# A new start for a fused feed-forward, attention and feed-forward kernel: loads, halving, bias and beta, and the orders of the first batch

## What is computed

```
ln(x)  = (x - mean) / sqrt(var + eps)
ffn(x) = (ln'(ln(x)) * gamma + beta) @ w_q.T + bias      # ln': once more, w_q = ternary(weight)
x = x + 0.5 * ffn(x)
x = x + attn(ln(x))          # 16 query heads, 4 key and value heads of 128, rotary positions,
                             # causal, window of 64, projection Wo, biases bq, bk, bv, bo
x = x + 0.5 * ffn(x)
```

## Time and profile before

| | |
|---|---|
| Median of 3 runs | 799.77 us (799.43 to 799.82) |
| The profiled execution | 799.18 us, of it 797.4 us span |
| TensorE busy | 782.2 us, 98% of the span |
| VectorE, ScalarE, GpSimd busy | 624.6, 468.2, 459.6 us |
| Mean granted TensorE clock | 0.993 |

### The profile page before, as it was taken

How to read it: one execution, slowest core, us unless ns; L and a number is a source line. 1 busy time by engine, 2 the same in 40 slices (tenths; PEclk the granted TensorE clock), 3 DMA queues, 4 the chain that set the end, 5 groups by cost and what they waited for, 6 DMA issues and landing times.

```text
span 797.4 us, 16145 instructions
## 1 busy us (share of the span) xinstructions
PE 782.2 (98%) x5658; PEld 731.4 (92%) x5658; DVE 624.6 (78%) x1325; ACT 468.2 (59%) x1595; POOL 459.6 (58%) x470
## 2 busy tenths in 40 slices
PE   6999999999999999999999999999999999999997
PEld 5788999999999999999999999999999999999996
DVE  4778967978679886888778887797867988687756
ACT  3176565656646576465656556465664657655573
POOL 3668743866357664467446674476635766446343
PEclk7999999999999999999999999999999999999999
DMA  8292425333243422524244242533324342243400
GB/s 297 53 232 62 94 50 137 80 94 80 54 120 93 126 48 58 154 67 109 52 97 116 64 110 53 134 81 87 86 55 120 93 121 52 54 106 75 113 14 27
DMA packets 54353, 74.11 MB, mean 93 GB/s; under 512 B 7168, under 2 KB 30208, under 8 KB 54272
## 3 DMA queue, kind: packets, MB, share of 16 engines
q1 hardware_dynamic: 53712, 72.74, 37.1%
q10 hardware_dynamic: 560, 0.34, 0.1%
HBM read 14.33 MB, written 4.19 MB: 23 GB/s over the span
## 4 chain that ended last, share of the span: by engine, by line
PE 93%; DVE 3%; issue 1%; POOL 1%; DMA 1%; ACT 1%; ACTq 0%; POOLq 0%; DVEq 0%
PE job_p L649 32%; PE attn_p L649 23%; PE scores_p L666 13%; PE heads_p L649 11%; PE probsT_p L728 7%; PE job_p L823 4%; PE job_p L801 2%; DMA columns_s<-columns 1%; PE job_p L814 1%; POOL q_s L1233 0%; DVE q_s L932 0%; PE heads_p L867 0%; ACT probs L1106 0%; DVE parts L998 0%; POOL probs L1222 0%
## 5 line engine op out<-in xcount | busy, mean ns | idle before, releaser
L649 PE MATMUL attn_p<-wo_s,headsT 128*128 128x256 f32 x1536 | 209.0, 286 | 1.5 <-ACT headsT L1127 1.5
L649 PE MATMUL job_p<-xnT,wq_s 128*128 128x512 f32 x768 | 205.9, 403 | 0.8 <-DVE v_s L938 0.5
L649 PEld LDWEIGHTS attn_p<-wo_s,headsT 128*128 128x128 f32 x1536 | 196.4, 190 | 7.2 <-ACT headsT L1127 2.2
L1106 ACT ACTIVATE probs<-scores_p,neg_max 128x96 f32<-128x96 f32 x512 | 168.0, 352 | 53.4 <-DVE neg_max L887 53.4
L1233 POOL TENSOR_TENSOR q_s<-q_s,rope_swap 128x512 f32<-128x512 f32 x128 | 164.2, 1291 | 47.8 <-DMA rope_swap<-rope_sin 47.5
L1222 POOL TENSOR_TENSOR probs<-probs,inv_sum 128x384 f32<-128x384 f32 x128 | 107.2, 838 | 140.8 <-DVE inv_sum L893 140.8
L1127 ACT ACTIVATE headsT<-heads_p,columns_s 128x512 fp32r<-128x512 f32 x128 | 88.2, 689 | 134.7 <-PE heads_p L649 134.3
L649 PEld LDWEIGHTS job_p<-xnT,wq_s 128*128 128x128 f32 x768 | 135.7, 189 | 26.2 <-DVE k_s L932 1.1
L921 DVE SCALAR_TENSOR_TENSOR rope_sin<-job_p,columns_s,rope_t 128x512 f32<-128x512 f32 x160 | 119.1, 744 | 21.8 <-PE job_p L649 21.4
L666 PE MATMUL scores_p<-k_s,q_s 128*128 128x96 f32 (+2 forms) x1024 | 131.6, 272 | 0.0
L666 PEld LDWEIGHTS scores_p<-k_s,q_s 128*128 128x128 f32 x1024 | 126.7, 192 | 2.5 <-POOL q_s L1233 0.2
(11 more groups left out here) (91 smaller groups left out, 981.7 us busy)
## 6 DMA issues: line engine op xcount, KB each, us to landing
rope_swap<-rope_sin SPq DMA_DIRECT2D x320, 128.0 KB, 2.4
v_odd<-v_s SPq DMA_DIRECT2D x64, 192.0 KB, 3.3
x_in<-x SPq DMA_DIRECT2D x15, 256.0 KB, 3.4
out<-x_res SPq DMA_DIRECT2D x15, 256.0 KB, 2.5
x_tr<-x_transposed SPq DMA_DIRECT2D x7, 512.0 KB, 5.3
q_s<-wq SPq DMA_DIRECT2D x3, 512.0 KB, 10.3
q_s<-wo SPq DMA_DIRECT2D x2, 512.0 KB, 10.6
x_res<-wo SPq DMA_DIRECT2D x2, 512.0 KB, 5.9
```

The source lines that it names most:

```text
L649: mm = nc.tensor.matmul(dst, a(p), b(q), start=clears and i == 0, stop=len(pairs) == 1, skip_group_check=True)
L1106: ins = nc.scalar.activation(probs[:, i, k, 0:REACH], scores_p[i][:, k, 0:REACH], ACT.Exp, bias=neg_max[:, i, k:k + 1], accum_out=row_sum[ ...
```

## The change

- ScalarE issues the columns first, then x_in blocks 2 and 3, then the identity.
- ScalarE halves gamma (gamma0i); beta is no longer halved. GpSimd loses gamma0i, half0i and the bias step of half 0.
- ScalarE makes y of batch 0, both halves, from shift and rstd. The one semaphore y_ready becomes two, one for each half of the y buffer.
- The beta matmuls in the banks of the first batch are gone. One product in attn_p sums bias (by the identity) and beta (by the ternary weights), ahead of the first FO. VectorE reads it: bias_first adds half of it to half 0 of x_in, fold_beta writes half of it to half_b. GpSimd adds half_b to half 1 as before.
- The tables of the prologue and of the first batch are new for all engines, the fills are (10, 2, 1, 3, 3). The tables of the middle and last batches are unchanged.

```diff
-FILLS = (10, 1, 1, 2, 6, 6)
+FILLS = (10, 2, 1, 3, 3)
...
+FIRST_BIASED = numbered(DVE_STEPS, "bias1")
...
-        y_ready = sem("y_ready")
+        y_ready = [sem(f"y_ready{i}") for i in range(2)]
...
                     else:
-                        pe.wait_ge(bias_ready, 2)
+                        pe.wait_ge(bias_ready, 1)
+                        if FIRST_BIASED:
+                            pe.wait_ge(first_biased, len(FIRST_BIASED))
...
-                if x[2] == 0 and x[0] == "FO1":
-
+                if FFN_OUT[x] == 0:
 
                     pe.wait_ge(tern_ready, 1)
-                    for k in range(2):
-                        for e in range(EC):
-                            nc.tensor.matmul(bank[:, k * E:(k + 1) * E], beta_s[:, e:e + 1].to_broadcast([P, P]),
-                                             w_tern[:, e, :].bitcast(F32), start=k == 0 and e == 0, stop=False,
-                                             skip_group_check=True)
...
             def beta_product(_):
 
+                pe.wait_ge(ident_in, 16)
+                pe.wait_ge(rows_in, 16)
+                nc.tensor.matmul(attn_p[0][:, 0, :], identf[:, :], half_b, start=True, stop=False)
+                pe.wait_ge(columns_in, 16)
                 pe.wait_ge(tern_ready, 1)
-                pe.wait_ge(gamma_ready, 1)
                 for e in range(EC):
                     mm = nc.tensor.matmul(attn_p[0][:, 0, :], beta_s[:, e:e + 1].to_broadcast([P, P]),
-                                          w_tern[:, e, :].bitcast(F32), start=e == 0, stop=e == EC - 1)
+                                          w_tern[:, e, :].bitcast(F32), start=False, stop=e == EC - 1)
                 mm.then_inc(beta_ready, 1)
...
                 dve.wait_ge(beta_ready, 1)
-                dve.wait_ge(biased["1"], 2)
-                nc.vector.tensor_tensor(half_b, attn_p[0][:, 0, :], half_b, ALU.add).then_inc(bias_ready, 1)
+                nc.vector.tensor_scalar(half_b, attn_p[0][:, 0, :], 0.5, None, ALU.mult).then_inc(bias_ready, 1)
+
+            def bias_first(x):
+
+                m = x[1]
+                wait_y(dve, Y_HALVES["YT1", m, 0])
+                dve.wait_ge(beta_ready, 1)
+                nc.vector.scalar_tensor_tensor(
+                    out=x_in[:, 2 * m:2 * m + 2, :], in0=attn_p[0][:, 0:1, :].to_broadcast([P, 2, E]), scalar=0.5,
+                    in1=x_in[:, 2 * m:2 * m + 2, :], op0=ALU.mult, op1=ALU.add).then_inc(first_biased, 1)
...
+            def halve_gamma(_):
+
+                act.wait_ge(columns_in, 16)
+                nc.scalar.activation(gamma_s, gamma_s, ACT.Copy, scale=0.5).then_inc(gamma_ready, 1)
...
+            act.dma_start(columns_s[:, :], columns).then_inc(columns_in, 16)
             act.dma_start(x_in[:, 2:4, :], x_t[0][:, 2:4, :]).then_inc(x_loaded[1], 16)
             act.dma_start(identf[:, :], ident).then_inc(ident_in, 16)
-            act.dma_start(columns_s[:, :], columns).then_inc(columns_in, 16)
...
-            def halve_gamma(_):
-
-                pool.wait_ge(columns_in, 16)
-                nc.gpsimd.tensor_scalar(gamma_beta, gamma_beta, 0.5, None, ALU.mult).then_inc(gamma_ready, 1)
-
-            def halve_bias(_):
-                pool.wait_ge(rows_in, 16)
-                nc.gpsimd.tensor_scalar(half_b, half_b, 0.5, None, ALU.mult).then_inc(bias_ready, 1)
```

In the first batch's tables SyncE loads x_tr ahead of the swap of key 1 and x_in behind that of query 6; TensorE has S3 ahead of O0 and Q9 ahead of T2; GpSimd has pad0i behind the rope additions and Q7 ahead of probs2; ScalarE has w9 ahead of w11:

```diff
     "first": """
-        K1c loadt0n Q4c load0n Q5c Q6c stage9f Q7c K2c Q8c Q9c Q10c Q11c K3c
+        loadt0n K1c Q4c Q5c Q6c load0n Q7c K2c stage9f Q8c Q9c Q10c Q11c K3c
```

More of the change, by code:

```diff
@@ L61 @@
     "prologue": """
-        fill0i total0i fill1i YT0n YT1n fill2i FO0n fill3i FO1n gsum0i open0i fill4i XT0n beta0i
-        fill5i XT1n V00n K0n Q0n Q1n Q2n Q3n V01n
+        fill0i total0i fill1i YT0n YT1n beta0i FO0n gsum0i fill2i FO1n open0i fill3i XT0n fill4i
+        XT1n V00n K0n Q0n Q1n Q2n V01n Q3n
     """,
     "first": """
-        K1c Q4c Q5c S0c S1c Q6c V10c T0c Q7c W0c T1c S2c O0c S3c
-        K2c W1c Q8c T2c Q9c S4c O1c V11c W2c T3c Q10c S5c O2c W3c
-        T4c S6c Q11c O3c W4c K3c Q12c T5c S7c O4c W5c T6c FO0n S8c
-        Q13c O5c W6c Q14c T7c O6c S9c FO1n W7c Q15c T8c XT0n O7c S10c
-        W8c T9c XT1n S11c O8c K0n W9c Q0n T10c O9c V00n W10c S12c Q1n
-        T11c O10c S13c Q2n W11c T12c S14c O11c W12c V01n T13c S15c Q3n O12c
+        K1c Q4c Q5c S0c S1c Q6c V10c T0c Q7c W0c T1c S2c S3c O0c
+        K2c W1c Q8c Q9c T2c V11c S4c O1c W2c T3c Q10c O2c S5c W3c
+        T4c S6c Q11c K3c O3c W4c T5c S7c O4c Q12c W5c T6c S8c FO0n
+        O5c Q13c W6c T7c Q14c S9c O6c FO1n W7c Q15c XT0n T8c O7c S10c
+        W8c T9c S11c XT1n O8c K0n W9c V00n T10c Q0n O9c S12c W10c Q1n
+        T11c S13c O10c Q2n W11c T12c S14c O11c W12c T13c S15c V01n Q3n O12c
         W13c T14c
@@ L355, in block_kernel @@
                                              for i in range(len(COLUMNS)))
-        gamma_beta = columns_s[:, sum(COLUMNS[:3]):]
         parts = sb("parts", [P, BLOCKS, 6])
@@ L498, in block_kernel, with wait_y @@
         WO_PIECE = (7, 9, 11, 12)
+        def wait_y(engine, n):
+            engine.wait_ge(y_ready[n % 2], n // 2 + 1)
         def wait_split(engine, *pieces):
@@ L794, in transpose_y @@
                 wait_for_bank(x)
-                pe.wait_ge(y_ready, Y_HALVES[x] + 1)
+                wait_y(pe, Y_HALVES[x])
                 if Y_HALVES[x] == 0:
@@ L823, in ffn_job @@
                             mm = nc.tensor.matmul(bank[:, k * E:(k + 1) * E], lnT[:, r, s, e, k * P:(k + 1) * P],
-                                                  w_tern[:, e, :], start=k == 0 and e == 0 and s == 0 and (x[2] > 0 or x[0] != "FO1"),
+                                                  w_tern[:, e, :], start=k == 0 and e == 0 and s == 0,
                                                   stop=e == EC - 1 and s == 1, skip_group_check=True)
@@ L961, in ffn_out @@
                     dve.wait_ge(centered, CENTERED["center", m, b] + 1)
+                elif ("bias1", m, b) in FIRST_BIASED and kind == "FO1":
+                    dve.wait_ge(first_biased, FIRST_BIASED["bias1", m, b] + 1)
                 else:
@@ L1150, in normalize @@
                                                scale=rstd[:, at:at + 1])
-                ins.then_inc(y_ready, 1)
+                ins.then_inc(y_ready[n % 2], 1)
             def values_high(x):
@@ L1191, in _ @@
                  "norm1": normalize, "norm2": normalize, "norm3": normalize, "anorm": normalize, "V": values_high, "XT": xn_high,
-                 "YT1": ffn_in_high, "YT2": ffn_in_high, "YT3": ffn_in_high, "w": split_high, "abs": sum_magnitudes}[x[0]](x)
+                 "YT1": ffn_in_high, "YT2": ffn_in_high, "YT3": ffn_in_high, "w": split_high, "abs": sum_magnitudes,
+                 "gamma": halve_gamma}[x[0]](x)
         @block.gpsimd
@@ L1243, in bias_residual @@
                 else:
-                    pool.wait_ge(y_ready, Y_HALVES["YT" + kind[-1], m, b] + 1)
-                pool.wait_ge(bias_ready, 1 if kind == "bias1" and b == 0 else 2)
+                    wait_y(pool, Y_HALVES["YT" + kind[-1], m, b])
+                pool.wait_ge(bias_ready, 1)
                 nc.gpsimd.tensor_tensor(buf[:, blocks, :], buf[:, blocks, :],
@@ L1302, in _ @@
                  "K": rope_add, "Q": rope_add, "bias1": bias_residual, "bias2": bias_residual, "bias3": bias_residual,
-                 "residual": residual, "half": halve_bias, "pad": pad, "gamma": halve_gamma,
+                 "residual": residual, "pad": pad,
                  "offset": mean_offset, "center": center, "w": split_low}[x[0]](x)
```

52 lines of the change are left out of this document (26 added, 26 removed).

## The result

| | before | after |
|---|---|---|
| Median of the runs shown together | 799.64 us (799.43 to 799.82) | 793.49 us (792.61 to 793.66) |
| Ratio, 95% interval | 1 | 0.9921 (0.9904 to 0.9938) |
| Profiled execution (span) | 799.18 us (797.4) | 793.66 us (791.9) |

The medians give 6.2 us, the interval 5.0 to 7.7, the two profiled spans 5.5. The forecast was 8.8 us and 791.0, with a range from 788.8 to 794.2 that holds 793.49.

What follows compares the result with a forecast made beforehand. The start was taken as the bound: rstd behind the columns' load, then TensorE's work. Scores 9.0 us earlier, less 0.9 lost, plus 0.7 gained, gave 8.8 us: 790.4 profiled, 791.0 with the median's 0.6; range 788.8 to 794.2.

## What to carry to other kernels

A gain at the front is only kept if the next stages have no wait of their own: draw the new time through every buffer's last reader, and list what each instruction's neighbour engine runs at that moment. Keep TensorE busy through gaps of the start with work that nobody reads: nine more fills were worth 3 us here, more than moving y or any load within the changed kernel. And when a start has three loads on one queue, put third what is needed last, since in all traces here the third was the latest.
